# Turning rows by transposing DMAs instead of by TensorE in the Mamba half of a two-part layer

## The chip, the cores and the metric

The kernel runs on one core of a Trainium2 chip. The metric is the device time of one execution in microseconds (us), of which the kernel before has three: median 3758.88, from 3757.54 to 3760.82.

## The reference

An input of 8 sequences of 1024 tokens with 512 features is normalised and goes through two blocks, whose results are added to it. The first is a Mamba-2 block, the second a routed attention that picks 512 queries and 256 keys for each of 4 groups. The change touches only the first:

```python
u = _layernorm(x, ln_w, ln_b)
zxbcdt = u @ in_proj_w.T
...
y = y * jax.nn.silu(z)
y = y * jax.lax.rsqrt(jnp.mean(y * y, -1, keepdims=True) + EPS) * gamma
return x + y @ out_proj_w.T
```

Both matrix products need their left operand with the features on the partitions. The rows, though, are normalised with the tokens on the partitions. So a block of rows is turned (transposed) ahead of each product: `u` ahead of the input projection, and the gated and normalised `y` ahead of the output projection.

## The kernel before

The Mamba half works through 16 blocks of 512 tokens, each of 4 chunks of 128 tokens: 64 chunks in all. Numbers that enter a product in full precision are split into two fp16 tiles, a high and a low part, and the product is the sum of three fp16 products.

For each chunk, `xn` normalises 128 rows, `xh` (ScalarE) and `low` (VectorE) write the two halves of the tile `xh` (128 x 2 x 512, two buffers). `turn` is 8 TensorE transposes of 128 x 128 into a PSUM bank, and `turn_out` a ScalarE copy to `xhT`. When the four chunks of a block are there, `logits`, ten `conv` products (one for each 128 channels, followed by four taps on VectorE) and `z` (two for each chunk) read `xhT`.

The scan itself is done by chunk: `open` turns the convolved channels, `inter` applies the state, `intra` is the product within the chunk, `state` makes the new state. `intra` of chunk ch needs the matrix `de[ch % 2]`, which is a broadcast of the cumulated decays over all partitions, read from DRAM by `bc_in` (1 MB, on the SP queue); `bc_in` of chunk ch waits for `intra` of chunk ch - 2. After `intra` comes a chain over three engines: `y2` and `yz` (VectorE), `square` (ScalarE), `mean` (VectorE), `root` (GpSimd), `y_high` (ScalarE), `y_low` (VectorE). It ends in the tile `yhl` (128 x 2 x 1024 fp16, one buffer). `gate` is 16 TensorE transposes of it into two PSUM banks, `gate_out` a ScalarE copy to `yT` (one buffer), and `proj` the output projection, 24 matrix products that read `yT`.

Every engine works through one fixed list of steps. The list is made before the launch: `make_plan` writes down the order of TensorE steps, and `arrange_steps` gives every step an engine, a duration, the steps that it needs, and an `extra` for what passes until a DMA has landed. `Order.run` then lists the steps of all engines by due time; TensorE may take one of the next four steps (`AHEAD_M`). On the chip nothing is reordered: an engine whose next step lacks its operand waits on a semaphore, and all behind it on that engine waits too. That holds for SP, which only issues DMAs, as well. In the Mamba half its list holds `x_in` (the rows of a block, 1 MB, which waits until `skip_store` of the block before has landed), `skip_store` and `rows_out` (1 MB each, to DRAM), `cum_store` and `bc_in`. Beside it GpSimd issues one accumulating DMA of 256 KB a chunk (`o_add`).

After the Mamba half (to about 1855 us of 3758) come a ranking of tokens and the attention half, in which nothing is changed.

Of the kernel before, what the change touches and what calls it, by code (L numbers as in the profile page):

```python
# [8 lines left out]
F32 = mybir.dt.float32  # L9
# [34 lines left out]
TURNS = CK * 3.45 + 15.23  # L44
CONV_START, CONV_END = -0.05, 1.05
# [318 lines left out]
def chain(*gens):  # L364
# [10 lines left out]
    "turn": [("single", 1, 1.4)],  # L375
# [15 lines left out]
    "turn": [(1.0, "turn_out")],  # L391
# [19 lines left out]
    "turn": lambda i, c: (("low", i, c), 1.5),  # L411
# [39 lines left out]
def arrange_steps(order, line, late):  # L451
# [3 lines left out]
    def last(step):  # L455
        return step if step[1] >= 0 else None
# [8 lines left out]
    for step in line:  # L465
# [3 lines left out]
        elif name == "turn":  # L469
            add("PE", 0.45, step, [("low", a, b)], [("single", [("turn_out", a, b)])])  # L470
        elif name == "logits":
            add("PE", 1.33, step, [("turn_out", a, c) for c in range(CK)] + [("slice_low", 0)], [("single", [("logits_out", a)])])
        elif name == "cum":
            add("PE", 1.9, step, [("dt", a)], [("single", [("cum_copy", a)]), ("single", [("cum_exp", a)])])
        elif name == "conv":
            add("PE", 2.6, step, [("turn_out", a, CK - 1), ("slice_low", PIECE_OF[b])], [("single", [("raw", a, b)])])
# [5 lines left out]
        elif name == "z":  # L482
            add("PE", 3.02, step, [("turn_out", a // CK, CK - 1), ("slice_low", 3 + b), ("bias_get", 3 + b)], [("single", [("z_silu", a, b)])])
        elif name == "gate":
            add("PE", 0.9, step, [("y_low", a)], [("pair", [("gate_out", a)])])
# [4 lines left out]
        elif name == "proj":  # L490
            add("PE", 5.18, step, [("gate_out", a), ("wout_low", KI - 1)], [("single", [("proj_out", a)])])
# [19 lines left out]
    for i in range(NBLK):  # L511
# [8 lines left out]
        for c in range(CK):  # L520
# [8 lines left out]
            add("ACT", 0.58, ("turn_out", i, c), [("turn", i, c)] + [last(("z", CK * (i - 2) + CK - 1, 1))])  # L529
# [18 lines left out]
    for ch in range(NCH):  # L548
# [12 lines left out]
        add("DVE", 1.22, ("dxs", ch), [("open", ch), ("bias_get", len(PIECES) - 1), ("slice_low", len(PIECES) - 1), last(("y2" if opens(ch - 1) else "y_skip", ch - 1))])  # L561
# [22 lines left out]
        add("ACT", 1.0, ("gate_out", ch), [("gate", ch), last(("proj", ch - 1))])  # L584
# [147 lines left out]
def make_plan():  # L732
# [6 lines left out]
    def norms(i):  # L739
        for c in range(CK):  # L740
            yield ("xn", i, c)
            yield Pause(3.0)
            if c:
                yield ("turn", i, c - 1)
                yield 0.6
        yield Pause(2.0)
        yield ("turn", i, CK - 1)
        yield 0.6

    def turns(i):  # L750
        for c in range(CK):
            yield ("turn", i, c)
            yield 0.45
            yield Pause(3.0)
        yield ("logits", i)
        yield 1.33
        yield Pause(12.0)
        yield ("cum", i)
        yield 1.9
# [6 lines left out]
    def back(i):  # L766
        for ch in range(i * CK, (i + 1) * CK):
# [23 lines left out]
            yield ("gate", ch)  # L791
            yield 0.9
# [6 lines left out]
    record.steps += [("slice_bias", 0), ("turn", 0, 0), ("turn", 0, 1), ("turn", 0, 2), ("turn", 0, 3),  # L799
# [100 lines left out]
class Sems:  # L900


    def __init__(self, sem):
        def two(name):
# [12 lines left out]
        self.turned, self.xT, self.skip_out, self.row_out = (sem(s) for s in ("x_turned", "xT", "skip_out", "row_out"))  # L917
# [18 lines left out]
        self.yh, self.yl, self.yt_mm, self.yT, self.o_mm, self.o = (  # L936
            sem(s) for s in ("y_high", "y_low", "y_turned", "yT", "o_mm", "o"))
# [22 lines left out]
def program(nc, x, w_in, ln_w, ln_b, conv_w, conv_b, a_log, d_skip, dt_bias, gamma, w_out,  # L960
            w_route, wq, wkv, wo, null_k, null_v, null_tok, consts, out):
    ctx = ExitStack()
    with ctx:
# [158 lines left out]
        def staged(g, k):  # L1122
# [19 lines left out]
            "turn": lambda i, c: [(S.xT, CK * i + c + 1)],  # L1142
# [6 lines left out]
            "gate": lambda ch: [(S.yT, ch + 1)],  # L1149
# [42 lines left out]
        def tensor_engine():  # L1192
# [25 lines left out]
            def turn(i, c):  # L1218
                q.wait_ge(S.xl, CK * i + c + 1)
                wait_given_back(q, "turn", i, c)  # L1220
                b16 = bank("turn", i, c)[:].bitcast(F16)
                for j in range(2 * KD):
                    ins = pe.transpose(b16[:, j * P:(j + 1) * P], xh[c % 2][:, j // KD, (j % KD) * P:(j % KD + 1) * P], id16[:])
                ins.then_inc(S.turned, 1)
# [1322 lines left out]
```

## Time and profile before

| | before |
|---|---|
| median of three runs | 3758.88 us |
| profiled execution | span 3758.3 us; the page gives no other time for it, and the median of the runs is 0.6 us above |
| Mamba half | 0 to 1855 us, 64 chunks |
| steady period (two blocks, 8 chunks) | 225.4 us |
| TensorE, VectorE, ScalarE busy in that period | 220.05, 198.31, 164.43 us |
| granted TensorE clock in that period | 1.00 of 2.4 GHz |

Busy time is the time in which at least one instruction of the engine was running. In the steady state the picture repeats every two blocks, so that one period of 225.4 us (900.1 to 1125.5 us, chunks 28 to 35) stands for the rest; the half has eight of them, less what differs at its two ends.

### The profile page before, as it was taken

The page shows a single profiled execution, that of the slowest core. Times are in us where ns is not written, and L with a number is a line of the kernel's source. Part 1 is how long each engine was busy: PE and PEld are TensorE (multiplying, and loading weights), DVE is VectorE, ACT ScalarE, POOL GpSimd, SP SyncE. Part 2 cuts the span into 40 slices and gives each one's busy share as a digit, 9 for nine tenths or more (in the row PEclk, how much of TensorE's full clock was granted, in tenths as well). Part 3 has the DMA queues.
Part 4 walks back from the last instruction along what each step waited for, and adds up shares of the span by engine and source line. Part 5 has one row for each costly group of instructions (what it writes and reads, how often), then busy time and mean ns, then how long its engine had stood idle before and what let it go on. Part 6 is the DMA issues. An engine that isn't in the chain of part 4 may idle for free.

```text
span 3758.3 us, 72452 instructions
## 1 busy us (share of the span) xinstructions
PE 3570.5 (95%) x28408; PEld 2173.2 (58%) x28408; DVE 2968.7 (79%) x5336; ACT 2534.8 (67%) x4777; POOL 1858.1 (49%) x1483
## 2 busy tenths in 40 slices
PE   7899999999999999999869999999999999999998
PEld 4555555555555555555435566556666566666665
DVE  6898988988889888988978777786777777677764
ACT  6677676777777767775637666676666766666665
POOL 1332333333333333332337887876665765666565
PEclk9899999999999999999979999999999999999999
DMA  4233322233332332322354343444333533333332
GB/s 144 60 89 79 87 58 74 69 88 79 79 77 65 77 80 77 85 60 55 73 86 119 63 82 69 75 106 86 73 79 69 111 80 76 71 74 78 74 68 38
DMA packets 297669, 294.29 MB, mean 78 GB/s; under 512 B 38663, under 2 KB 222087, under 8 KB 295280
## 3 DMA queue, kind: packets, MB, share of 16 engines
q1 hardware_dynamic: 241008, 186.70, 19.8%
q0 software_dynamic: 56320, 102.94, 15.4%
q8 instruction: 226, 3.70, 0.4%
q14 instruction: 115, 0.94, 0.1%
HBM read 176.19 MB, written 101.71 MB: 74 GB/s over the span
## 4 chain that ended last, share of the span: by engine, by line
PE 64%; DVE 14%; ACT 3%; issue 3%; DMA 2%; POOL 1%; another core or an unknown queue 0%; SPq 0%; ACTq 0%; DVEq 0%
PE pair L1384 8%; PE pair L1499 6%; PE pair L1336 6%; PE pair L1250 5%; PE pair L1298 5%; PE pair L1399 4%; PE pair L1413 4%; PE pair L1346 3%; PE pair L1460 3%; PE pair L1459 3%; PE pair L1429 2%; DVE cv L1649 2%; PE pair L1480 2%; PE pair L1478 2%; PE pair L1488 2%
## 5 line engine op out<-in xcount | busy, mean ns | idle before, releaser
L2345 POOL TENSOR_TENSOR ph<-pf,ph 128x512 f16<-128x512 f32 x256 | 381.7, 1492 | 319.2 <-ACT ph L2208 316.4
L1649 DVE SCALAR_TENSOR_TENSOR cv<-raw,taps,cv 128x512 f32<-128x512 f32 x480 | 417.7, 892 | 19.7 <-ACT cv L2062 18.0
L1903 DVE TENSOR_REDUCE smx<-pair 128x2 f32<-128x514 f32 x512 | 349.9, 685 | 82.1 <-PE pair L1429 79.1
L1250 PE MATMUL pair<-xhT,whi 128*128 128x512 f16 x1280 | 382.0, 380 | 5.8 <-DVE dts L1607 5.7
L1298 PE MATMUL pair<-zhi,xhT 128*128 128x512 f16 x1024 | 331.4, 385 | 13.7 <-DVE yb L1727 10.7
L2202 ACT ACTIVATE pf<-pair 128x1024 f32<-128x1024 f32 x256 | 262.1, 1024 | 96.0 <-PE pair L1460 92.2
L1336 PE MATMUL pair<-ohi,yT 128*128 128x512 f16 x1024 | 320.2, 384 | 3.3 <-ACT yT L2120 3.3
L2092 ACT ACTIVATE de<-de,cum 128x128 f32<-128x128 f32 x1024 | 311.2, 388 | 1.1
L1938 DVE TENSOR_TENSOR ph<-pf,ph 128x512 f16<-128x512 f32 x256 | 232.2, 908 | 99.4 <-ACT ph L2208 98.2
L2208 ACT CAST ph<-pf 128x1024 f16<-128x1024 f32 x256 | 267.9, 1047 | 4.4
L1346 PEld LDWEIGHTS pair<-xdt,de 128*128 128x128 f32 x2048 | 250.7, 201 | 17.8 <-issue 10.6
L1346 PE MATMUL pair<-xdt,de 128*128 128x64 f32 x2048 | 249.6, 283 | 9.3 <-issue 5.6
L2350 POOL TENSOR_TENSOR ohl<-of,ohl 128x256 f16<-128x256 f32 x256 | 200.8, 793 | 86.0 <-ACT ohl L2213 83.9
L1865 DVE SCALAR_TENSOR_TENSOR qa<-pair,qa 64x512 f16<-64x512 f32 x256 | 176.5, 689 | 84.5 <-ACT qa L2173 79.2
L1250 PE MATMUL pair<-xhT,wlo 128*128 128x512 f16 x640 | 243.1, 380 | 0.0
L2339 POOL DMA_INDIRECT y<-res,slot_i x128 | 214.0, 1672 | 51.7 <-ACT res L2227 31.9
L1480 PE MATMUL pair<-vhi,ph 128*128 128x65 f16 x2048 | 238.3, 194 | 0.0
L1478 PE MATMUL pair<-vhi,ph 128*128 128x65 f16 x2048 | 238.3, 194 | 0.0
L1479 PE MATMUL pair<-vlo,ph 128*128 128x64 f16 x2048 | 237.8, 193 | 0.0
L2318 POOL DMA_INDIRECT gat<-rows,slot_i x192 | 193.8, 1009 | 63.1 <-issue 28.7
L2276 POOL TENSOR_TENSOR yb<-yb,dxs 128x1024 f32<-128x1024 f32 x56 | 150.4, 2685 | 141.2 <-DVE yb L1700 139.8
L1476 PE MATMUL pair<-nvb,pnT 96*128 96x65 f16 x1024 | 200.3, 196 | 11.4 <-ACT xq L2165 7.3
(273 smaller groups left out, 10462.2 us busy)
## 6 DMA issues: line engine op xcount, KB each, us to landing
de<-cum SPq DMA_DIRECT2D x64, 1024.0 KB, 9.4
rows<-rowt SPq DMA_DIRECT2D x16, 1040.0 KB, 4.2
xin<-x SPq DMA_DIRECT2D x16, 1024.0 KB, 13.6
y<-xin SPq DMA_DIRECT2D x16, 1024.0 KB, 4.3
y<-ob POOLq DMA_DIRECT2D x64, 256.0 KB, 4.4
qb<-qa SPq DMA_DIRECT2D x32, 512.0 KB
rbc<-rank SPq DMA_DIRECT2D x63, 256.0 KB
wst<-wkv SPq DMA_DIRECT2D x32, 256.0 KB
```

The source lines that it names most:

```text
L1250: ins = pe.matmul(bk[:], w[:, k, ws], xt[:, ha, k, :], start=n == 0, stop=n == 3 * KD - 1)
L1298: pe.matmul(pz[:], xt[:, ha, k, cs], w[:, k, j * 512:(j + 1) * 512], start=n == 0, stop=False)
L1336: ins = pe.matmul(bk[:], yT[:, ha * KI + k, :], w[:, k, :], start=k == 0 and n == 0, stop=k == KI - 1 and n == 2)
L1346: ins = pe.matmul(pw[:, h * HD:(h + 1) * HD], de[ch % 2][:, h, :], xdt[:, h, :], start=True, stop=True)
L1384: ins = pe.matmul(bk[:], w[:, k, ws], xq[:, ha * KD + k, :], start=n_ == 0, stop=n_ == 3 * KD - 1)
L1478: pe.matmul(o, p_[:, 0, j, qs_], vhi[u][:, j, h, :], start=False, stop=False, skip_group_check=True)
L1480: ins = pe.matmul(o, p_[:, 1, j, qs_], vhi[u][:, j, h, :], start=False, stop=j == KT - 1, skip_group_check=True)
L1649: ve.scalar_tensor_tensor(c_[:], r_[:, t:t + BLK], taps[:, ct, t:t + 1], c_[:], ALU.mult, ALU.add).then_inc(done, 1)
L1903: ve.tensor_reduce(smx[:, qt, 2 * h2:2 * h2 + 2], sc[:, :, 0:NK + 1], AX.X, ALU.max)
L2092: ins = ac.activation(d_[:, h, :], d_[:, h, :], ACT.Relu, bias=cum_t[i % 2][:, c, h:h + 1], scale=-1.0)
L2208: ac.copy(p_[:, 0], f[:]).then_inc(S.ph, 1)
L2345: po.tensor_tensor(p_[:, 1, 1], f[:, 1], p_[:, 0, 1], ALU.subtract).then_inc(S.plp, 1)
```

## The change

The steps `turn` and `gate` move from TensorE to SP. Each is now one transposing DMA from SBUF to SBUF: of `xh`, 128 x 1024 fp16 (256 KB), to `xhT`; and of `yhl`, 128 x 2048 fp16 (512 KB), to `yT`. The 64 x 8 and 64 x 16 TensorE transposes, the PSUM banks that they used, and the ScalarE copies `turn_out` and `gate_out` are gone. Who waited for a transpose or a copy now waits for the landing of the DMA: `xh` for the transposing DMA of two chunks before, `square` for that of the chunk before, `logits`, `conv` and `proj` for their operands. Two waits that the old steps implied are written out (`xdt` for `xw`, `gram_out` for `mask`). The planner is told that issuing takes 0.6 us, and landing a further 4.0 and 5.0 us; the lists of all engines are made anew from that.

```diff
+TURN_ISSUE, TURN_LANDS, GATE_LANDS = 0.6, 4.0, 5.0
...
-        elif name == "turn":
-            add("PE", 0.45, step, [("low", a, b)], [("single", [("turn_out", a, b)])])
...
-        elif name == "gate":
-            add("PE", 0.9, step, [("y_low", a)], [("pair", [("gate_out", a)])])
...
-            add("PE", 5.18, step, [("gate_out", a), ("wout_low", KI - 1)], [("single", [("proj_out", a)])])
+            add("PE", 5.18, step, [("gate", a), ("wout_low", KI - 1)], [("single", [("proj_out", a)])])
...
-            add("ACT", 0.58, ("turn_out", i, c), [("turn", i, c)] + [last(("z", CK * (i - 2) + CK - 1, 1))])
+            add("SP", TURN_ISSUE, ("turn", i, c), [("low", i, c), last(("z", CK * (i - 2) + CK - 1, 1))], extra=TURN_LANDS)
...
-        add("ACT", 1.0, ("gate_out", ch), [("gate", ch), last(("proj", ch - 1))])
+        add("SP", TURN_ISSUE, ("gate", ch), [("y_low", ch), last(("proj", ch - 1))], extra=GATE_LANDS)
...
             def conv(i, ct):
-                q.wait_ge(S.xT, CK * (i + 1))
+                for j in range(2):
+                    q.wait_ge(S.xT[j], 16 * CK // 2 * (i + 1))
...
             def proj(ch):
-                q.wait_ge(S.yT, ch + 1)
+                q.wait_ge(S.yT, 16 * (ch + 1))
...
+                q.wait_ge(S.xw, kept(ch))
...
             def gram_out(ch):
                 q.wait_ge(S.g, ch + 1)
+                q.wait_ge(S.m, ch)
...
             def xh_(i, c):
                 ch = CK * i + c
                 q.wait_ge(S.xn, ch + 1)
-                q.wait_ge(S.turned, ch - 1)
+                q.wait_ge(S.xT[c % 2], 16 * (ch // 2))
...
             def square(ch):
                 q.wait_ge(S.yz, ch + 1)
-                q.wait_ge(S.yt_mm, ch)
+                q.wait_ge(S.yT, 16 * ch)
...
-            def gate_out(ch):
-                q.wait_ge(S.yt_mm, ch + 1)
-                q.wait_ge(S.o_mm, ch)
-                ac.copy(yT[:].bitcast(F32).rearrange("p j t -> p (j t)"), bank("gate", ch)[:]).then_inc(S.yT, 1)
...
+            def turn(i, c):
+                q.wait_ge(S.xl, CK * i + c + 1)
+                q.wait_ge(S.z_mm, 2 * CK * (i - 1))
+                sp.dma_start_transpose(xhT[i % 2][:].rearrange("p h k t -> p (h k) t")[:, :, c * P:(c + 1) * P],
+                                       xh[c % 2][:].rearrange("p h d -> p (h d)")).then_inc(S.xT[c % 2], 16)
+
+            def gate(ch):
+                q.wait_ge(S.yl, ch + 1)
+                q.wait_ge(S.o_mm, ch)
+                sp.dma_start_transpose(yT[:], yhl[:].rearrange("p h d -> p (h d)")).then_inc(S.yT, 16)
```

How the lists of steps change shows at two places. The first is the SP list about chunks 29 to 33. `de<-cum` is `bc_in`, `rows<-rowt` is `rows_out`, `cum<-cumT` is `cum_store`, `xhT<-xh` is `turn` and `yT<-yhl` is `gate`. Of the kernel before (`bc_in` of chunks 29 to 33):

```order
L2408 DMA de<-cum 128x16x128
L2389 DMA xin<-x 128x4x512
L2398 DMA rows<-rowt 128x4x520
L2408 DMA de<-cum 128x16x128
L2402 DMA cum<-cumT 16x512
L2408 DMA de<-cum 128x16x128 x2
L2393 DMA y<-xin 128x4x512
L2408 DMA de<-cum 128x16x128
```

Of the changed kernel (`bc_in` of chunks 30 to 33, `gate` of chunks 28 to 31, the four `turn` of block 9):

```order
128 L2371 DMA de<-cum 128x16x128
129 L2361 DMA rows<-rowt 128x4x520
130 L2352 DMA_TRANSPOSE yT<-yhl 128x16x128
131 L2365 DMA cum<-cumT 16x512
132 L2371 DMA de<-cum 128x16x128
133 L2352 DMA_TRANSPOSE yT<-yhl 128x16x128
134 L2371 DMA de<-cum 128x16x128
135 L2346 DMA_TRANSPOSE xhT<-xh 128x8x128 x2
136 L2352 DMA_TRANSPOSE yT<-yhl 128x16x128
137 L2346 DMA_TRANSPOSE xhT<-xh 128x8x128 x2
138 L2371 DMA de<-cum 128x16x128
```

Between two `bc_in` there now stand one `gate` and, in one gap of each block, up to four `turn` as well. In six of the blocks `x_in` (`xin<-x`) comes right behind a `bc_in`, with the next `gate` behind both; this is the place at `bc_in` of chunks 17 and 18, with `gate` of chunk 15:

```order
80 L2346 DMA_TRANSPOSE xhT<-xh 128x8x128 x2
81 L2356 DMA y<-xin 128x4x512
82 L2371 DMA de<-cum 128x16x128
83 L2341 DMA xin<-x 128x4x512
84 L2352 DMA_TRANSPOSE yT<-yhl 128x16x128
85 L2361 DMA rows<-rowt 128x4x520
86 L2371 DMA de<-cum 128x16x128
```

The second place is ScalarE, in the changed kernel, from `square` of chunk 30 (row 929) to the last two `xh` of block 9 (rows 944 and 947), which wait for the first two `turn` of SP row 135:

```order
936 L2071 ACTIVATE yhl<-yb,yn 128x1024
937 L2018 ACTIVATE cv<-raw,conv_bias,taps 128x512
938 L2060 ACTIVATE zs<-pair 128x512
939 L1971 CAST rowt<-xn 128x512
940 L1996 ACTIVATE xsT<-cv 128x512
941 L1981 ACTIVATE xin<-xin,nrm 128x512
942 L2076 ACTIVATE ob<-pair 128x512
943 L2038 COPY btok<-pair 128x128
944 L1977 ACTIVATE xh<-xn,nrm 128x512
945 L1966 ACTIVATE xn<-xin,nrm 128x512
946 L1996 ACTIVATE xsT<-cv 128x512
947 L1977 ACTIVATE xh<-xn,nrm 128x512
```

In the kernel before, the third `xh` of that block waited for TensorE alone; now it stands some ten instructions behind `y_high` of chunk 30 (row 936) and waits for a DMA.

## Rows read from the trace of the kernel before

**Rows 1.** The page: busy time and share by engine; granted clock in slices.

```profile
PE 3570.5 (95%) x28408; PEld 2173.2 (58%) x28408; DVE 2968.7 (79%) x5336; ACT 2534.8 (67%) x4777; POOL 1858.1 (49%) x1483
...
PEclk9899999999999999999979999999999999999999
```

**Rows 2.** Busy time by stretch: Mamba half, one steady period, the ranking behind.

```profile
0.00:1855.00 1855.00, 1770.38 (x10763) 1043.77 (x10764) 1599.06 (x2248) 1318.54 (x2933) 598.71 (x393) 0.98 0.32 78
900.10:1125.50 225.40, 220.05 (x1365) 128.62 (x1363) 198.31 (x268) 164.43 (x366) 76.02 (x49) 1.00 0.32 76
1855.00:2020.00 165.00, 121.15 (x802) 72.20 (x801) 131.19 (x257) 77.79 (x131) 77.33 (x68) 0.80 0.49 93
```

**Rows 3.** Waits of TensorE, 200 to 1800 us: first and last of eleven.

```profile
PE pair L1298 <- DVE yb L1727: 10.7, 5, 2.1
...
PE pair L1307 <- DVE dxs L1684: 0.2, 1, 0.2
```

**Rows 4.** Timeline about one `gate` (L1307) and one `turn` (L1223).

```profile
930.37 1.06 PE L1307 MATMUL pair<-id,yhl 128*128 128x128 f16 x16
931.26 0.59 PE L1250 MATMUL pair<-xhT,whi 128*128 128x512 f16 x2
931.46 1.01 ACT L2120 COPY yT<-pair 128x1024 f32<-128x1024 f32 x1 [3.60 <-PE pair L1307]
...
985.53 0.61 PE L1223 MATMUL pair<-id,xh 128*128 128x128 f16 x8
985.97 0.71 PE L1275 MATMUL pair<-cst,xsT 128*128 128x128 f32 x5
```

**Rows 5.** Groups of ScalarE in the Mamba half: the two copies.

```profile
L2120 ACT COPY yT<-pair 128x1024 f32<-128x1024 f32 x61 | 61.5, 1008 | 64.0 <-PE pair L1307 63.7
L2025 ACT COPY xhT<-pair 128x512 f32<-128x512 f32 x64 | 36.6, 573 | 7.3 <-PE pair L1223 7.3
```

**Rows 6.** Timeline: `intra` (L1346) of chunk 28, three `y_low` (L1741), their `proj` (L1336).

```profile
914.49 3.68 PE L1346 MATMUL pair<-xdt,de 128*128 128x64 f32 x32
927.58 1.28 DVE L1741 SCALAR_TENSOR_TENSOR yhl<-yb,yn,yhl 128x1024 f16<-128x1024 f32 x1
934.84 0.38 PE L1336 MATMUL pair<-ohi,yT 128*128 128x512 f16 x1
...
1013.49 1.28 DVE L1741 SCALAR_TENSOR_TENSOR yhl<-yb,yn,yhl 128x1024 f16<-128x1024 f32 x1
1021.96 0.38 PE L1336 MATMUL pair<-ohi,yT 128*128 128x512 f16 x1
...
1120.43 1.28 DVE L1741 SCALAR_TENSOR_TENSOR yhl<-yb,yn,yhl 128x1024 f16<-128x1024 f32 x1
1130.56 0.39 PE L1336 MATMUL pair<-ohi,yT 128*128 128x512 f16 x1
```

**Rows 7.** DMA, 200 to 1800 us: SP's queue; issues with KB, us to landing.

```profile
q1 hardware_dynamic: 140800, 103.98, 24.1%
...
de<-cum SPq DMA_DIRECT2D x57, 1024.0 KB, 9.4
...
rows<-rowt SPq DMA_DIRECT2D x14, 1040.0 KB, 4.2
...
xin<-x SPq DMA_DIRECT2D x13, 1024.0 KB, 13.6
...
cum<-cumT SPq DMA_DIRECT2D x14, 32.0 KB, 1.6
```

**Rows 8.** Timeline of SP: a `bc_in`, an `x_in`; landing of all `x_in`.

```profile
886.95 0.36 SPq L2408 DMA_DIRECT2D de<-cum  x1
887.35 1.92 SPq L2389 DMA_DIRECT2D xin<-x  x1
...
DMA to landing us min/median/max: 5.1/13.6/15.1
```

**Rows 9.** Waits in the first 150 us: TensorE for `low` of block 0.

```profile
PE pair L1223 <- DVE xh L1596: 18.5, 5, 5.0
```

More of the change, by code:

```diff
@@ L468, in arrange_steps @@
             add("PE", 4.9 if a > 2 else 3.5, step, [("slice_in", a)], [("single", [("bias_get", a)])])
-        elif name == "turn":
-            add("PE", 0.45, step, [("low", a, b)], [("single", [("turn_out", a, b)])])
         elif name == "logits":
-            add("PE", 1.33, step, [("turn_out", a, c) for c in range(CK)] + [("slice_low", 0)], [("single", [("logits_out", a)])])
+            add("PE", 1.33, step, [("turn", a, c) for c in range(CK)] + [("slice_low", 0)], [("single", [("logits_out", a)])])
         elif name == "cum":
@@ L475, in arrange_steps @@
         elif name == "conv":
-            add("PE", 2.6, step, [("turn_out", a, CK - 1), ("slice_low", PIECE_OF[b])], [("single", [("raw", a, b)])])
+            add("PE", 2.6, step, [("turn", a, CK - 1), ("slice_low", PIECE_OF[b])], [("single", [("raw", a, b)])])
         elif name == "gram":
@@ L737, in feed @@
         return Feed(gen, total, plan, alone)
[L739 to L748, printed above, removed]
     def turns(i):
[L751 to L754, printed above, removed]
+        yield Pause(CK * 3.45)
         yield ("logits", i)
@@ L1241, in conv @@
             def conv(i, ct):
[L1242 removed]
+                for j in range(2):
+                    q.wait_ge(S.xT[j], 16 * CK // 2 * (i + 1))
                 q.wait_ge(S.wlo_m, PIECE_OF[ct] + 1)
@@ L1300, in z @@
                 pe.matmul(pz[:], ones[:], z_bias[:, j * 512:(j + 1) * 512], start=False, stop=True).then_inc(S.z_mm, 1)
-            def gate(ch):
-                q.wait_ge(S.yl, ch + 1)
-                wait_given_back(q, "gate", ch)
-                pt16 = bank("gate", ch)[:].bitcast(F16)
-                for j in range(2 * KI):
-                    ins = pe.transpose(pt16[:, j * P:(j + 1) * P], yhl[:, j // KI, (j % KI) * P:(j % KI + 1) * P], id16[:])
-                ins.then_inc(S.yt_mm, 1)
             def inter(ch):
@@ L2478, in stored @@
                     q.wait_ge(S.res_out[j], 16 * ITEMS * QT // 2)
-            does = {"prep": prep, "slice_in": slice_in, "wout_in": wout_in, "x_in": x_in,
+            does = {"prep": prep, "slice_in": slice_in, "wout_in": wout_in, "x_in": x_in, "turn": turn, "gate": gate,
                     "skip_store": skip_store, "rows_out": rows_out, "cum_store": cum_store, "bc_in": bc_in,
```

43 lines of the change are left out of this document (11 added, 32 removed).

## The prediction

> **What bounds the kernel now.** I read the page first: TensorE is busy for 95% of the span, VectorE for 79%, ScalarE for 67%, and nearly every slice has the full clock [rows 1]. Then busy time by stretch, since the change touches only the Mamba half: there TensorE is busy 1770 of 1855 us. In one steady period it is 220.05 of 225.4 us, VectorE 198.31 (88%) and ScalarE 164.43 (73%), at a granted clock of 1.00 [rows 2]. Third, who TensorE waits for: the longest of eleven releasers costs 10.7 us in 1600, the shortest 0.2, and all eleven together 35 us [rows 3]. So TensorE is the bound, and what is taken from it is gained, as long as the thing that takes its place is not late; VectorE is the next bound, 27 us of idle time per period behind.
>
> **What is removed.** The end of a busy time is modelled, so I price a step by the distance from its start to the start of the next TensorE step. A `gate` starts at 930.37 and its follower at 931.26: 0.89 us. A `turn` starts at 985.53, its follower at 985.97: 0.44 us [rows 4]. There are 64 of each: 64 x (0.89 + 0.44) = 85 us. ScalarE loses 64 copies of 1.008 us and 64 of 0.573 us [rows 5], 101 us; it waits a lot already, and this makes room and does not count by itself.
>
> **What it costs VectorE.** Its work stays 198.3 us, while the period would fall by 8 x 1.33 = 10.6 us to 214.8: its idle time falls from 27.1 to 16.5 us [rows 2]. TensorE's own idle time is 5.35 us per period now. If that grows as VectorE's idle time shrinks, it becomes 5.35 x 27.1 / 16.5 = 8.8 us, 3.4 more. The freed banks and ScalarE's room work against that, so I take half: 1.7 x 8 periods = +14 us (ends: 0 and +28).
>
> **How long the transposing DMAs take.** No row shows one. Below: the smallest DMA of SP, 32 KB, lands in 1.6 us, and 1040 KB go out in 4.2 us, so 1008 KB cost 2.6 us; by bytes `gate` (512 KB) is 1.6 + 1.3 = 2.9 us, and `turn` (256 KB) 2.3. Above, as an estimate: `bc_in` writes 128 x 16 = 2048 runs of 512 B, and `gate` has 2048 runs of 256 B if it is cut into runs of 128 elements. SP's queue took 24.1% of 16 engines in 1600 us for 140800 packets, 43.8 ns each, so 2048 of them are 5.6 us on 16 engines, and the other 3.8 of the 9.4 us are the fixed part. By runs `gate` takes 9.4 us, and `turn` with half as many 6.6 [rows 7]. A transpose has to write narrow pieces, so it is nearer to `bc_in`: I take 7.0 and 5.0 us, plus 0.36 us to issue (as `bc_in`, rows 8).
>
> The pages pull both ways. The Trainium skill ("Advanced Engine Details and Errata", X-Bar Transpose) has transposing DMAs as fast as plain ones, 350 to 400 GB/s; by it `gate` would be at my lower end. The Trainium skill ("VectorE: DVE Perf Modes", the three transpose paths) has 1309 ns for 128 x 128 by DMA against 390 by TensorE, and advises TensorE where PSUM will do; 16 such tiles in a row would be 20.9 us, and the sum below would end near 4500 us. No row here decides between them.
>
> **What hides it.** What matters is how long after the end of `y_low` its `proj` starts. In the period of [rows 6] the eight distances are 5.98, 6.86, 9.39, 7.19, 6.44, 9.37, 14.55 and 8.85 us (first, fourth and last stand there: 927.58 + 1.28 = 928.86 to 934.84, and so on). TensorE works on other steps meanwhile, so these are slack. A landing after 7.4 us is late by 1.42, 0.54, 0.21 and 0.96 us in four of eight: 3.1 us per period, 25 us in all. At 9.8 us seven are late by 14.5 us in sum: 116 us in all. At 3.3 us none is. The new list helps a little: the TensorE steps between `intra` and `proj` of a chunk, 16.4 us or more in the old list, are 17.7 or more in the new one (estimates, with step durations of this trace). I take +15 of the 25.
>
> **What stands in SP's queue.** SP's DMAs go out one behind another: the `x_in` issued 0.4 us behind a `bc_in` is one of thirteen whose median landing is 13.6 us, while the quickest took 5.1 [rows 8]; 13.6 is about 9.4 + 4.2. `bc_in` is issued when `intra` ends, at 918.2 in [rows 6]; `y_low` ends 10.7 us later, just behind its landing. So a lone `gate` meets an empty queue, and that cover is thin. (a) In six blocks `x_in` stands between the two: it lands 14.0 us after `bc_in` was issued, `gate` is 3.3 us later. Less the slack of some: +10 us. (b) In most blocks two `turn` go out right behind a `bc_in` with a `gate` behind them (SP rows 134 to 136 in the change). Two transfers of 1.6 us (half of 7.0 less the fixed 3.8) end 12.6 us after the issue, so `gate` is 1.9 us later in some 14 blocks, of which slack hides half: +12 us. (c) Behind these `turn` wait the third and fourth `xh` on ScalarE: row 944 is reached some 13 us after `intra`, the first `turn` lands at about the same time. If it is later, `raw`, `decs` and `de` behind it on ScalarE are late, and with them `mask` and the next `intra`. At 5.0 us I take nothing. (d) SP now waits for `y_low` ahead of the next `bc_in`; that one is needed a chunk later (28 us), and costs nothing. (e) `square` waits for the `gate` before, 24 us earlier: nothing. (f) The written-out waits of `xdt` and `gram_out` are for steps long done: nothing.
>
> **The start.** TensorE waits 18.5 us for `low` in block 0 [rows 9]; now a landing follows each, the last uncovered: +5 us.
>
> **Sum.** -85 + 14 + 15 + 10 + 12 + 5 = -29 us, from the profiled 3758.3 (0.6 below the median of the runs): about 3730 us, 0.8% faster. The likeliest case alone: 3690 to 3755.
>
> **Rivals.**
> 1. *The landing is short* (3 to 4 us): no distance is missed, the queue terms vanish. -85 + 14 + 5 and some 6 of queueing = -60: 3699 us. For it: bytes by [rows 7]. Chance 0.15.
> 2. *The transposes run by runs like `bc_in`, or a little worse.* 116 less 20 for the new order, queue terms doubled to 45: -85 + 14 + 96 + 45 + 5 = +75: about 3833 us, with 3750 to 3890 around it. It decides from a landing of about 8.5 us on. For it: the run count; against: half the bytes. Chance 0.21.
> 3. *The transposes go tile after tile instead of 16 at a time.* Sixteen tiles at 1.6 us, what the smallest DMA takes [rows 7], are 25.6 us. Every `proj` waits: 139 us per period by the eight distances, 1114 us in all, about 4800 us; half as long a landing (13.2 us) still adds some 300, about 4000 us. Past 24 us `square` waits too, as `yhl` has one buffer. The clock may add to it: behind the Mamba half, where TensorE is busy for 121 of 165 us, the granted clock is 0.80 [rows 2]. By the second of the two pages this is the case to expect. Chance 0.18.
> 4. *VectorE is already the bound.* If its 27 us of idle time per period can't shrink, the period stays 225 us and only waits move: 3759 us. Against it: TensorE's waits are 35 us in 1600 [rows 3]. Chance 0.08.
>
> My forecast keeps 0.38. A change of less than 0.2% (7.5 us) can't be told from none here. Faster: 0.35 of the forecast, 0.15 of rival 1 and 0.01 of rival 2: 0.51. Within 0.2%: 0.02, rival 4 and 0.02 of rival 2: 0.12. Slower: 0.01, 0.18 and 0.18: 0.37. The range of 3680 to 3890 takes in rival 2 and leaves 0.18 above it and 0.02 below.
>
> **What will show it.** The issue table gives `gate` and `turn` with us to landing: 7.0 and 5.0, or not; this alone decides most. TensorE's waits should name the DMA `yT` as what `proj` waits for, 20 to 60 us in sum, and the DMA `xhT` with next to nothing. The steady period should be near 222 us (225.4 less 29 / 8), TensorE busy 209.5 of it, VectorE 198. ScalarE's wait for the `turn` DMA ahead of `xh` should be small. A clock below 1.00 in the steady state, or an SP issue of some us for each transpose, would break the sum: SP would then be late with `bc_in` as well.

## The result, and the profile after

The changed kernel takes 3690.69 us (median of four runs, 3684.36 to 3697.4) beside 3759.85 us of the kernel before (four runs, 3757.54 to 3766.13). The ratio is 0.9816, with a 95% interval of 0.9801 to 0.9831: 1.8% faster, some 69 us. The forecast was 3730 us: the direction was right, and the gain is 2.4 times the 29 us that it had. One of four executions of a kernel below (`gate` alone) took 7336.86 us, twice the others, and is left out of its median and ratio.

The page of the changed kernel: span; busy time, share and instructions by engine; granted clock in slices.

```profile
span 3690.6 us, 69594 instructions
...
PE 3470.4 (94%) x26872; PEld 2075.7 (56%) x26872; DVE 2934.9 (80%) x5336; ACT 2445.5 (66%) x4649; POOL 1871.1 (51%) x1483
...
PEclk9899999999999999999879999999999999999999
```

Against [rows 1] TensorE has lost 100 us and 1536 matmuls (64 x 24), ScalarE 89 us. VectorE has lost 34 us with the same number of instructions. Two of its groups in the Mamba half became shorter, by 29 us each: `low`, and the product that ends the SiLU behind the convolution (`xsT`). Their medians are as before (0.75 and 0.68 us); there are fewer long cases (of up to 2.9 us). Why, no run here shows. The first line of each pair is the kernel before:

```profile
L1596 DVE SCALAR_TENSOR_TENSOR xh<-xn,nrm,xh 128x512 f16<-128x512 f32 x64 | 90.4, 1413 | 30.0 <-ACT xh L2014 30.0
L1557 DVE SCALAR_TENSOR_TENSOR xh<-xn,nrm,xh 128x512 f16<-128x512 f32 x64 | 61.7, 965 | 6.7 <-ACT xh L1977 6.4
...
L1655 DVE SCALAR_TENSOR_TENSOR xsT<-xsT,cv 128x512 f32<-128x512 f32 x160 | 157.2, 987 | 32.8 <-ACT xsT L2040 32.5
L1616 DVE SCALAR_TENSOR_TENSOR xsT<-xsT,cv 128x512 f32<-128x512 f32 x160 | 128.2, 813 | 9.4 <-ACT xsT L1996 8.0
```

Busy time by stretch (columns as in [rows 2]): the Mamba half, 220 us of the steady state, and the ranking behind.

```profile
0.00:1820.00 1820.00, 1708.40 (x9400) 968.28 (x9401) 1600.70 (x2303) 1247.76 (x2842) 626.60 (x402) 0.98 0.49 108
900.00:1120.00 220.00, 217.45 (x1213) 122.56 (x1212) 199.22 (x281) 153.13 (x352) 88.94 (x53) 1.00 0.48 106
1820.00:1990.00 170.00, 116.07 (x907) 69.35 (x906) 129.00 (x265) 85.16 (x136) 90.53 (x82) 0.84 0.58 111
```

The DMA share has gone from 0.32 to 0.49. To place the gain I take the stretch from the start of the first `intra` to the start of the last (63 chunks on), before and after:

```profile
111.60:1899.30 1787.70, 1722.91 (x10512) 1011.47 (x10512) 1566.61 (x2165) 1260.26 (x2816) 599.39 (x388) 0.98 0.31 75
111.70:1820.10 1708.40, 1636.72 (x9039) 922.30 (x9040) 1525.05 (x2146) 1174.80 (x2688) 609.85 (x387) 0.98 0.48 106
```

TensorE was busy for 1722.9 us and idle for 64.8; now it is busy for 1636.7 and idle for 71.7. So its busy time fell by 86 us, its idle time grew by 7, and the stretch is 79 us shorter. From the last `intra` to the end it is the other way round: 1859.1 us before, 1870.5 after, so that some 12 us are given back there in this profile. In the profile of the same kernel once more (below) it is 1863.7, so only part of the 12 us is sure.

The clock did change. It has two levels, 1.00 (2.4 GHz) and 0.50 (1.2 GHz), and this is 200 to 1700 us in the profiles before, after, and with `gate` alone:

```profile
200.00:1700.00 1500.00, 1467.13 (x9122) 1.00 0.31 76
200.00:1700.00 1500.00, 1457.60 (x8141) 0.99 0.49 108
200.00:1700.00 1500.00, 1476.06 (x8564) 1.00 0.43 98
```

The clock records behind these means show it finer: the lower level was granted for 14 us in all before, for 37 us after (again 37 in the repeated run), and for 10 us with `gate` alone (14 in its repeated run). Each of the seven falls of the changed kernel comes during a wait of TensorE of 2 to 6 us or within 1.3 us of its end.

DMA between 200 and 1750 us: SP's queue, and issues with KB and median us to landing.

```profile
q1 hardware_dynamic: 319625, 149.62, 41.4%
...
de<-cum SPq DMA_DIRECT2D x58, 1024.0 KB, 9.5
...
xin<-x SPq DMA_DIRECT2D x13, 1024.0 KB, 9.2
...
yT<-yhl SPq DMA_TRANSPOSE x57, 4.3
xhT<-xh SPq DMA_TRANSPOSE x54, 3.8
```

Here is the row that the forecast said would decide most: `gate` lands in 4.3 us where 7.0 was taken, and `turn` in 3.8 where 5.0 was. `bc_in` still takes 9.5, and `x_in` has gone from 13.6 [rows 7] to 9.2, as it is issued 4.8 us or more behind a `bc_in` in 12 of 13 cases, where it was 0.4 us behind in 11 of 13. The same two steps by line, with the time that an issue keeps SP (min/median/max in ns), who waited for them, and the spread of the landings:

```profile
L2352 SPq DMA_TRANSPOSE yT<-yhl x57: 1322/1894/3949, 218.3 to 1723.2; - x57
...
  PE pair L1297: 12.3, 3
...
DMA to landing us min/median/max: 4.2/4.3/10.4
```
```profile
L2346 SPq DMA_TRANSPOSE xhT<-xh x54: 1232/1296/6160, 204.4 to 1610.4; - x54
...
  ACT xh L1977: 1.9, 1
...
DMA to landing us min/median/max: 2.7/3.8/10.0
```

The landing counts from the start of the issue, so the 1.9 us of issuing are within the 4.3. One `gate` in the timeline, from the end of `y_low` (1807.46 + 1.27) to the first matmul of `proj`, shows that: issued at 1808.76, read at 1813.07, 4.31 us later.

```profile
1807.46 1.27 DVE L1704 SCALAR_TENSOR_TENSOR yhl<-yb,yn,yhl 128x1024 f16<-128x1024 f32 x1
...
1808.76 1.79 SPq L2352 DMA_TRANSPOSE yT<-yhl  x1
...
1813.07 0.61 PE L1297 MATMUL pair<-ohi,yT 128*128 128x512 f16 x1 [11.44 <-DMA yT<-yhl]
...
1838.37 0.61 PE L1297 MATMUL pair<-ohi,yT 128*128 128x512 f16 x1 [14.61 <-DMA yT<-yhl]
...
1869.36 2.81 PE L1332 MATMUL pair<-id,gat 128*128 128x128 f16 x24 [22.19 <-DMA gat<-rows,slot_i]
```

The two `proj` here are the last of the half. TensorE has little else to do and waits 11.4 and 14.6 us. The landing is 4.3 us of each wait; the rest is the chain from `intra` to `y_low`, with no other work beside it. Then TensorE runs at 0.61 us a matmul where [rows 6] has 0.38: the granted clock was 0.50 from 1806.5 to 1816.7 and from 1827 to 1844 us. Only the second wait lies behind the last `intra` (1820.1), where the 12 us are. There the last landing (4.3 us) and the slow `proj` (8.2 us where 5.2 is usual) stand on the chain of work that ended last. Who TensorE waits for over the whole half (us in total, times, longest):

```profile
PE pair L1297 <- DMA yT<-yhl: 38.3, 5, 14.6
PE pair L1204 <- issue: 23.9, 6, 11.8
```

Of the 38.3 us for `yT`, 26.0 are those two chunks; the other 62 chunks cost 12.3 us, of which 11.9 are two waits. In both of these, SP had issued `bc_in`, `x_in` and then `gate`, and the `gate` landed only after 10.4 and 9.9 us:

```profile
536.62 0.51 SPq L2371 DMA_DIRECT2D de<-cum  x1
541.82 1.23 SPq L2341 DMA_DIRECT2D xin<-x  x1
548.46 3.95 SPq L2352 DMA_TRANSPOSE yT<-yhl  x1
...
558.87 0.61 PE L1297 MATMUL pair<-ohi,yT 128*128 128x512 f16 x1 [6.14 <-DMA yT<-yhl]
```

The second row is `logits` (L1204), which can start only when all four `turn` of a block have landed. Behind block 0 it waits for another 12.1 us in all, 9.1 of them at two places where the last `turn` of a block was issued some 2 us behind a `bc_in` and landed after 8.4 and 8.3 us:

```profile
315.45 0.37 SPq L2371 DMA_DIRECT2D de<-cum  x1
317.36 4.32 SPq L2346 DMA_TRANSPOSE xhT<-xh  x1
...
325.81 0.18 PE L1204 MATMUL pair<-shi,xhT 128*128 128x24 f16 x1 [4.56 <-issue]
```

The longest wait for `logits`, 11.8 us, is that of block 0 and stands where the 18.5 us of [rows 9] stood; the first `intra` starts at 111.7 us, as it did before (111.6).

### The profile page after: what moved, and what is told of

Its sections match the earlier page's. It is cut to its first block, busy times and chain, and to the rows that moved or that the text cites. A ratio compares the mean times of both kernels' runs of the same rounds, so it can differ in the third digit from the quotient of the medians.

```text
span 3690.6 us, 69594 instructions
## 1 busy us (share of the span) xinstructions
PE 3470.4 (94%) x26872; PEld 2075.7 (56%) x26872; DVE 2934.9 (80%) x5336; ACT 2445.5 (66%) x4649; POOL 1871.1 (51%) x1483
## 4 chain that ended last, share of the span: by engine, by line
PE 69%; DVE 14%; DMA 4%; issue 4%; ACT 3%; POOL 1%; another core or an unknown queue 0%; DVEq 0%; ACTq 0%
PE pair L1345 8%; PE pair L1297 7%; PE pair L1219 7%; PE pair L1460 6%; PE pair L1267 6%; PE pair L1360 4%; PE pair L1307 4%; PE pair L1374 4%; PE pair L1421 3%; PE pair L1420 3%; PE pair L1390 2%; PE pair L1278 2%; PE pair L1287 2%; PE pair L1441 2%; PE pair L1332 2%
## 5 line engine op out<-in xcount | busy, mean ns | idle before, releaser
L1610 DVE SCALAR_TENSOR_TENSOR cv<-raw,taps,cv 128x512 f32<-128x512 f32 x480 | 429.0, 921 | 27.8 <-ACT cv L2018 26.5
L1297 PE MATMUL pair<-ohi,yT 128*128 128x512 f16 x1024 | 322.5, 387 | 39.1 <-DMA yT<-yhl 38.3
L2153 ACT ACTIVATE pf<-pair 128x1024 f32<-128x1024 f32 x256 | 262.1, 1024 | 92.3 <-PE pair L1421 88.3
L1307 PEld LDWEIGHTS pair<-xdt,de 128*128 128x128 f32 x2048 | 239.7, 193 | 16.7 <-issue 8.7
L1307 PE MATMUL pair<-xdt,de 128*128 128x64 f32 x2048 | 237.7, 275 | 3.8 <-DVE dxs L1646 3.8
L2231 POOL TENSOR_TENSOR yn<-yn,neghalf 128x1 f32<-128x1 f32 x64 | 48.7, 760 | 350.3 <-DVE yn L1700 350.1
L1219 PEld LDWEIGHTS pair<-xhT,whi 128*128 128x128 f16 x1280 | 123.8, 99 | 168.9 <-issue 35.2
```

What stands on the lines that cost most here:

```text
L1219: ins = pe.matmul(bk[:], w[:, k, ws], xt[:, ha, k, :], start=n == 0, stop=n == 3 * KD - 1)
L1297: ins = pe.matmul(bk[:], yT[:, ha * KI + k, :], w[:, k, :], start=k == 0 and n == 0, stop=k == KI - 1 and n == 2)
L1307: ins = pe.matmul(pw[:, h * HD:(h + 1) * HD], de[ch % 2][:, h, :], xdt[:, h, :], start=True, stop=True)
L1610: ve.scalar_tensor_tensor(c_[:], r_[:, t:t + BLK], taps[:, ct, t:t + 1], c_[:], ALU.mult, ALU.add).then_inc(done, 1)
L2153: ac.activation(f[:].rearrange("p k q -> p (k q)"), bank("score", n, h)[:], ACT.Exp, scale=SCALE).then_inc(S.pf, 1)
```

## The experiments

Each ratio is against the kernel before on the same chip, with its 95% interval. Where two kernels are compared I take the difference of their ratios times 3760 us; an interval is some 6 us to either side, so a difference under about 8 us is not settled (12 where `gate` lands later with the lists not told of it: there the interval is 9 to 10 us to either side).

### One step alone

The first kernel keeps `gate` as a DMA and has `turn` and `turn_out` of the kernel before; the second is the reverse. The lists are made anew for each.

```diff
-                sp.dma_start_transpose(xhT[i % 2][:].rearrange("p h k t -> p (h k) t")[:, :, c * P:(c + 1) * P],
-                                       xh[c % 2][:].rearrange("p h d -> p (h d)")).then_inc(S.xT[c % 2], 16)
+                for j in range(2 * KD):
+                    ins = pe.transpose(b16[:, j * P:(j + 1) * P], xh[c % 2][:, j // KD, (j % KD) * P:(j % KD + 1) * P], id16[:])
```

> Only `gate` is a DMA, `turn` is back on TensorE and ScalarE. If the gain is the TensorE time removed (0.89 us for each of 64 gates, 57 us), less a few us of waits: 3705 to 3718. If the gain came from the emptier lists of ScalarE or from freed banks, no fixed share is expected; ScalarE loses 65 of the 101 us here, which would give about 3715 as well, so that this run alone does not tell the two apart.

> Only `turn` is a DMA. TensorE time removed: 64 x 0.44 = 28 us; with the landings of `turn` hidden: 3732 to 3742. If the `turn` landings hold up ScalarE at `xh`, as the forecast feared, or SP is late with `bc_in`: 3760 or more.

Measured: `gate` alone 3680.36 us (median of three), 0.9813 (0.9793 to 0.9833); `turn` alone 3713.84 us, 0.9893 (0.9876 to 0.9909). So `gate` alone gives 70 us and `turn` alone 40, and both together 69. Each alone gives more than I expected, and more than the TensorE time that it removes (57 and 28 us). They do not add up: on top of `gate`, moving `turn` gives nothing. The same kernel once more, beside the unaltered changed kernel on one chip:

> The kernel with only `gate` by DMA once more: 3685. If `turn` by DMA adds nothing on top of `gate` by DMA, it is within 0.3% of the changed kernel beside it; if engine time freed always counts (28 us of TensorE, 37 of ScalarE, at their prices some 20 us), it should be slower by 20 us.

> The changed kernel once more, unaltered, on the same chip as the two beside it: 3690, within 0.2%. It shows how far a repetition alone moves.

3686.36 us, 0.9806 (0.9792 to 0.9819), and 3689.96 us, 0.9817 (0.9804 to 0.9831): the same again. The stretch from first to last `intra` shows how it comes about. With `gate` alone it is this:

```profile
115.90:1816.30 1700.40, 1648.32 (x9447) 942.44 (x9443) 1551.41 (x2149) 1198.40 (x2746) 609.62 (x387) 0.99 0.43 97
```

TensorE is busy for 1648.3 us and idle for 52.1; with both it is busy for 1636.7 and idle for 71.7. Moving `turn` takes only 12 us off TensorE's busy time, and 20 us of idle time come back. In the half with `gate` alone, the wait for block 0 and that for `yT` look like this:

```profile
PE pair L1207 <- DVE xh L1572: 21.3, 5, 7.2
PE pair L1312 <- DMA yT<-yhl: 14.8, 5, 10.7
```

14.8 us for `yT` against 38.3. Between 200 and 1700 us it is 2.6 against 12.3, and `logits` waits for 0.3 us, against 12.1: these are the waits behind `bc_in` and `x_in` shown above. With them go 37 us at the lower clock against 10. TensorE does its work at half pace there, so that, as an estimate, up to (37 - 10) / 2 = some 13 us more of its busy time are the same work done slower. Together this is about what `turn` was worth. It was not tested by a run that changes only the order on SP at these places; the lists of the two kernels differ everywhere.

### The engines' work put back

In the changed kernel, with its lists and its DMAs, I put back the TensorE work alone: 24 transposes of 128 x 128 a chunk, into the bank of `z` ahead of its products, where nothing reads them.

```diff
             def z(ch, j):
...
+                pz16 = pz[:].bitcast(F16)
+                for m in range(12):
+                    pe.transpose(pz16[:, m % 8 * P:(m % 8 + 1) * P], id16[:], id16[:])
```

> The changed kernel with 12 spare TensorE transposes of the identity ahead of each `z` product, 24 a chunk, which nobody reads: TensorE's time is given back, ScalarE's is not. Theory that TensorE's time is the gain: back to 3755 to 3785 (3691 + 64 x 24 x 0.0555 = 85 us). Rival that ScalarE's room and the freed banks made it: stays under 3715.

Then ScalarE's alone: three copies of 128 x 512 a chunk.

```diff
             def z_tanh(ch, j):
...
+                for _ in range(2 - j):
+                    ac.copy(zs[:, j * 512:(j + 1) * 512], bank("z", ch, j)[:]).then_inc(*own.up())
+                    q.wait_ge(*own.now())
```

> The changed kernel with three spare ScalarE copies a chunk of a `z` bank (0.58 us each, 111 us in all; 101 were removed), each waited for by ScalarE itself. Theory that TensorE's time is the gain: 3691 to 3710. Rival that ScalarE's room made it: 3730 to 3760.

And both together:

> The changed kernel with both the spare TensorE transposes and the spare ScalarE copies. Alone they cost 46 and 27 us (ratios 0.9939 and 0.9887 against 0.9816). If the two are all there is in the gain and add up: 3755 to 3775. If the freed PSUM banks, the new lists or the absent wait of TensorE for ScalarE's copy are worth something by themselves: 3725 to 3745. If they cross: under 3735.

The groups show that the work is there (TensorE between 200 and 1700 us; ScalarE in the whole run):

```profile
L1267 PE MATMUL pair<-id 128*128 128x128 f16 x1308 | 90.8, 219 | 0.3 <-DVE zs L1659 0.3
```
```profile
L2061 ACT COPY zs<-pair 128x512 f32<-128x512 f32 x192 | 110.9, 578 | 11.0 <-PE pair L1269 8.9
```

Measured: TensorE's work back 3730.13 us, 0.9939 (0.9923 to 0.9956), 46 us above the changed kernel; ScalarE's back 3716.43 us, 0.9887 (0.9868 to 0.9907), 27 us above; both back 3762.58 us, 0.9997 (0.9986 to 1.0009), 68 us above, which is the size of the whole gain. 46 + 27 = 73 agrees with 68 within the intervals. I had expected the first to return all of it (3755 to 3785), and the second little or nothing (3691 to 3710): both were wrong. The transposing DMAs run in all three kernels, and the lists are those of the changed kernel. So at fixed lists the time of the two engines is worth about 0.54 us for each of TensorE's 85, and 0.24 for each of ScalarE's 111.

That this is the whole gain is not shown. The lists were not told of the spare work, and the order of the lists alone is worth some 20 us (below). VectorE's work did not come back: it is busy for 192.7 us in eight chunks with both works put back, where it was 197.2 before and is 191.7 in the changed kernel. The lower clock did go: 7 us between 200 and 1700 us with both put back and 10 with TensorE's work alone, against 37, which makes the spare work look cheaper than it is. And the two prices do not give the kernels with one step moved: by them `gate` would be worth 0.54 x 57 + 0.24 x 65 = 46 us and `turn` 0.54 x 28 + 0.24 x 37 = 24, where 70 and 40 were measured.

### VectorE, which the change leaves alone

`xdt` (1.22 us on VectorE) is computed twice in each chunk, in the changed kernel and in the kernel before.

```diff
+                ve.tensor_tensor(xdt[:], p3, dt_t[i % 2][:, c, :].unsqueeze(2).to_broadcast([P, NH, HD]), ALU.mult).then_inc(*own.up())
+                q.wait_ge(*own.now())
```

> The changed kernel with `xdt` computed twice on VectorE (1.22 us a chunk, 78 us in all). Theory that after the change VectorE is a bound beside TensorE (TensorE's time given back cost only half, so TensorE alone is not it): +35 to +70 us, 3725 to 3760. Theory that TensorE alone bounds: under +15, 3705.

> The same spare work in the kernel before. If TensorE was the bound there and VectorE had 27 us of idle time per period, as the forecast read it: +0 to +20 us, 3760 to 3780. If VectorE's wait chain counted there already: +35 to +70.

The doubled instruction in the kernel before:

```profile
L1677 DVE TENSOR_TENSOR xdt<-pair,dt 128x1024 f32<-128x1024 f32 x63 | 77.1, 1224 | 2.2
```

In the changed kernel it costs 48 us (3739.12 us, 0.9944, 0.9928 to 0.996), in the kernel before 41 (3801.76 us, 1.0108, 1.0091 to 1.0125), for 78 us put in: 0.62 and 0.53 a us. The two can't be told apart. So VectorE's 27 us of idle time in a period of 225 took up only about half of the work put in, in either kernel. The price is that of work at this place, ahead of `intra`, with lists that are not told of it.

### A later landing

A first transposing DMA, whose landing SP awaits, is put ahead of `gate`: of one 128 x 128 tile, then of all 16.

```diff
+                sp.dma_start_transpose(yT[:, 0:1, :], yhl[:].rearrange("p h d -> p (h d)")[:, 0:1 * P]).then_inc(S.yT0, 16)
+                q.wait_ge(S.yT0, 16 * (ch + 1))
                 sp.dma_start_transpose(yT[:], yhl[:].rearrange("p h d -> p (h d)")).then_inc(S.yT, 16)
```

> Each `gate` is issued only when a first transposing DMA, of one 128 x 128 tile of the same rows, has landed; so `yT` is there some 7 us after `y_low` and not 4.3. This is the landing that the forecast took. Slack read from the changed kernel's own trace (64 distances from `y_low` to `proj`, 4.34 to 11.5 us) is missed by 26 us in sum at 7.2 us: 3710 to 3725. The forecast's own sum for this landing was 3730. If the landing is not what set the time (rival: the forecast's terms for VectorE and for SP's queue were too high, and the landing mattered little): under 3700.

> The same with a first DMA of all 16 tiles, so that `yT` lands twice as late, at 8.7 us or so. By the distances, missed by 78 us in sum: 3755 to 3785. Rival that the landing mattered little: under 3720. Rival 2 of the forecast had 3833 for 9.8 us.

SP in the first of them, one `gate`; then TensorE's wait for `yT` in the half, in the first and in the second:

```profile
1027.24 1.13 SPq L2352 DMA_TRANSPOSE yT<-yhl  x1
1029.58 1.33 SPq L2354 DMA_TRANSPOSE yT<-yhl  x1
```
```profile
PE pair L1297 <- DMA yT<-yhl: 65.6, 20, 17.0
```
```profile
PE pair L1297 <- DMA yT<-yhl: 132.7, 52, 15.7
```

From `y_low` to `yT` it is now some 6.7 us with one tile (3724.57 us, 0.9902, 0.9874 to 0.9929: 32 us slower than the changed kernel), and some 8.9 with sixteen (median; 8.6 at least; 3845.82 us, 1.0218, 1.0193 to 1.0243: 151 us slower, and slower than the kernel before). The first comes close to the landing that the forecast assumed for `gate` (7.0 + 0.36 us; `turn` stays short), and 3724.57 us is near its 3730. The second is well above what I expected (3755 to 3785). The distances from `y_low` to `proj` in the changed kernel's timeline, 64 of them, are missed by 17 us in sum at 6.7 us and by 78 at 8.7. The runs gave about twice that. Only 27 and 94 us of it are in the wait for `yT`. The stretch from first to last `intra` shows more. The changed kernel stands above (1708.40 us, TensorE busy for 1636.72); here are the one with one tile and the one with sixteen:

```profile
111.80:1853.10 1741.30, 1645.66 (x9039) 925.07 (x9040) 1525.23 (x2150) 1175.76 (x2688) 611.21 (x387) 0.97 0.48 105
111.90:1962.90 1851.00, 1674.79 (x9038) 930.18 (x9039) 1521.80 (x2153) 1177.88 (x2688) 609.82 (x387) 0.96 0.54 116
```

TensorE's idle time grows by 24 and 104 us. Its busy time grows as well, by 9 and 38 us, with the same matmuls: the lower clock was granted for 48 and 102 us between 200 and 1700 us, where it was 37. So a quarter of what the late landing costs in this stretch is TensorE at the lower clock. Of the idle time, the part that is not in the wait for `yT` was not taken apart; SP is held for the first landing too, and so everything behind it in its list is later.

Then the same first DMA, with lists that are told of it (`GATE_LANDS` 6.7 instead of 5.0):

> The late `gate` (7 us, through a first DMA of one tile) with lists that are told of it (0.6 + 6.7 in place of 0.6 + 5.0). If a landing of 7 us can be hidden by another order: 3690 to 3705, in place of 3725. If the chain from `intra` to `proj` is simply too long for the work that is there: 3715 to 3730.

3693.2 us, 0.982 (0.9807 to 0.9834). TensorE's wait for `yT`:

```profile
PE pair L1297 <- DMA yT<-yhl: 26.7, 7, 12.7
```

The same later landing costs 32 us if the lists are not told. If they are, the kernel is as fast as the changed kernel; against the kernel with the same lists and the short landing (0.9795, the last one below) it is 0.0025 or 9 us slower, at the edge of what can be told.

### The lists alone

`GATE_LANDS`, `TURN_LANDS` and the time of issuing only decide in which order the engines' fixed lists are written. First the measured values (issue 1.8 and landing 2.5 for `gate`, 1.25 and 2.5 for `turn`, block 0 left as it was), with both steps as DMAs and with `gate` alone; then wide ones (1.8 and 5.5, 1.25 and 5.0); then 0.6 and 6.0 with `gate` alone; last 0.6 and 6.7 for `gate` in the changed kernel.

```diff
-TURN_ISSUE, TURN_LANDS, GATE_LANDS = 0.6, 4.0, 5.0
+TURN_ISSUE, TURN_LANDS, GATE_ISSUE, GATE_LANDS = 0.6, 4.0, 0.6, 6.7
...
-        add("SP", TURN_ISSUE, ("gate", ch), [("y_low", ch), last(("proj", ch - 1))], extra=GATE_LANDS)
+        add("SP", GATE_ISSUE, ("gate", ch), [("y_low", ch), last(("proj", ch - 1))], extra=GATE_LANDS)
```

> The changed kernel with lists made from the measured DMA times (`turn` 1.25 us to issue and 2.5 more to land, `gate` 1.8 and 2.5, from block 1 on) in place of 0.6 + 4.0 and 0.6 + 5.0. The work is the same. Theory that `turn` by DMA costs some 8 us of waits on top of `gate` by DMA only because the lists leave SP and the landing out of step: 3670 to 3685, faster than the only-gate kernel. Rival that the two together are at a floor set by VectorE: 3685 to 3700, no change.

> Only `gate` by DMA, lists made from its measured times. If lists matter little: 3675 to 3695, the same as the only-gate kernel (3685). If they are a lottery of their own: anything 15 us off.

> Both by DMA, lists made as if they landed late (`turn` 1.25 + 5.0, `gate` 1.8 + 5.5). Work and landings are the same. It measures how far the lists alone move the time: 3680 to 3700 if little. If TensorE's waits for `xhT` ahead of `logits` (12 us in the steady state) were the price of `turn` by DMA, they vanish and it gains about as much: 3675 to 3685.

> Only `gate` by DMA, with lists made as if it landed after 0.6 + 6.0 us; it lands after 4.3 in all. If a margin in the lists is what pays (the late landing told to the lists lost nothing, the lists with the tight measured times lost 29 us): 3670 to 3690. If the lists are only a lottery: anywhere from 3680 to 3715.

> The changed kernel, with lists made as if `gate` landed after 0.6 + 6.7 us: the lists of the late gate that was told, without its first DMA. If a margin ahead of `proj` is worth more than tightness: 3675 to 3690 (faster than the changed kernel beside it). If the time hangs on the lists only by chance and the landing is hidden either way: within 10 us of the late gate's 3693.

| lists | us | ratio (95%) |
|---|---|---|
| both steps, as measured | 3697.57 | 0.9842 (0.9829 to 0.9856) |
| `gate` alone, as measured | 3713.57 | 0.9875 (0.986 to 0.989) |
| both steps, wide | 3698.74 | 0.984 (0.9826 to 0.9853) |
| `gate` alone, 0.6 + 6.0 | 3701.2 | 0.984 (0.9823 to 0.9858) |
| both steps, `gate` 0.6 + 6.7 | 3682.02 | 0.9795 (0.9778 to 0.9812) |

With the same steps on every engine the ratio goes from 0.9795 to 0.9842 with both steps (18 us), and from 0.9806 and 0.9813 to 0.9875 with `gate` alone (23 to 26 us). The true durations give worse lists than the wrong ones, by 10 and 23 to 26 us, and the wider margins except the last are slower by 9 to 13 us as well. The last is the fastest kernel of all here, 2.05% below the kernel before; beside the changed kernel on the same chip it is 0.2% faster, with intervals that overlap.

## Why the prediction came out as it did

**The step that failed: how long the transposing DMAs take.** The forecast took 7.0 and 5.0 us, between an end by bytes (2.9 and 2.3) and an end by runs (9.4 and 6.6), "nearer to `bc_in`". They took 4.3 and 3.8. The landings count the issue. The number of runs was right: between 200 and 1700 us the queue carried 177,568 packets more than before, of which 6,144 belong to three more `bc_in`, and 55 `gate` of 2048 and 54 `turn` of 1024 make 167,936.

Two prices were wrong. The first is that of a run: the queue's share rose from 24.3% to 41.4% of 16 engines in those 1500 us, 4104 us for 177,568 packets, or 23 ns each. The forecast had 43.8, but that is the mean over all packets of the queue. In the trace the 512 B packets of `bc_in` took 36.3 ns before and 34.4 after, and the 256 B packets of the transposes 23.5 (21.3 where a `gate` ran alone). The second, and for the total as large, is the fixed part of 3.8 us, which was `bc_in`'s landing less its runs. A `gate` that runs alone has its first packet 1.2 us after the start of the issue, its packets take 2.6 us, and it has landed 0.5 us later: 1.7 us beside the runs. With 3.8 it would have been 6.4 us, still near the forecast. The packets of a `bc_in`, for their part, take 3.5 to 4.9 us of 16 engines and are mostly spread over about 8, so that its landing is not engine time plus a fixed part. The issue was put at 0.36 us and takes 1.9 and 1.3; it is within the landing.

The two pages fare as follows. By the Trainium skill ("Advanced Engine Details and Errata", X-Bar Transpose) a transposing DMA is as fast as a plain one. The trace does not agree for the rate: the packets of a `gate` alone move 512 KB in 2.6 us, some 200 GB/s, and those of a `rows_out` alone 1040 KB in 2.9 us, some 370. By the Trainium skill ("VectorE: DVE Perf Modes", the three transpose paths) 128 x 128 takes 1309 ns by DMA; the trace does not agree for 16 tiles in one DMA, 0.27 us each, nor for one tile by itself, which was there after 2.3 us (the run with one tile ahead of `gate`).

**What hangs on it.** With the short landing the term +15 (missed slack) has next to nothing left to price: apart from two waits behind `x_in`, TensorE waits for `yT` for 0.4 us in all between 200 and 1700 us. The two queue terms did not vanish. `x_in` ahead of `gate` (+10) cost 11.9 us of waits in two blocks. `turn` ahead of `gate` (+12) cost `proj` nothing, but `turn` behind `bc_in` kept `logits` waiting for 9.1 us, a place where the forecast saw no cost. The run with nearly the landing that the forecast assumed gave 3725 us, 32 above the changed kernel, where the three terms are 31 above the 6 of rival 1. The size is right, but only the landing of `gate` was moved there, and the two queue terms are for other places than those where the trace shows waits, so part of the agreement is luck. Rival 1's case, -85 + 14 + 5 + 6 = -60 and 3699 us, is 8 above what was measured. Rival 2's case was reached by the run with sixteen tiles ahead of `gate`: with 8.9 us behind `y_low` the kernel is 82 us slower than before, where the forecast had it break even at 8.5 and 75 us slower at 9.8. Between the points at 6.7 and 8.9 it would break even at some 7.4 us (an estimate, on a straight line), so the forecast held a late landing too cheap; the lower clock, a quarter of the cost above, was in no term of its rival 2. The later landing costs less once the lists are told of it, which the forecast did not count: it took the slack of the old lists as given, when the planner makes it.

**TensorE's work, -85 us.** As busy time it was right: 86 us are gone. As a price it was too high, and ScalarE's 101 us at nothing were too low: 46 and 27 us by the runs with the work put back at fixed lists. The two errors nearly cancel, so that -85 is near the 69 us for a wrong reason. The second step that failed is this one: ScalarE's time "does not count by itself". Rival 4 (VectorE is already the bound) was wrong as the case in which nothing is gained, and right in that VectorE's time counts: over half a us for each us, before the change too. So "TensorE is the bound, VectorE the next" was the wrong reading of [rows 2, 3]: work on each of three engines costs time.

**VectorE's idle time, +14 us.** TensorE's idle time in the half grew by 7 us for all causes together, and from 5.2 to 5.8 us in eight chunks (chunks 8 to 56). That VectorE's work stays the same did not hold: it fell from 197.2 to 191.7 us in eight chunks, by the shorter groups above. At the measured 0.5 to 0.6 this would be worth some 20 us of the gain (an estimate), which no term had.

**The start, +5 us.** The first `intra` starts when it did before: nothing. The longer tail at the other end, 12 us and 5 in the two profiles, was in no term; an uncovered landing and a `proj` at the lower clock are in it.

**The signs.** The table of issues decided, as foretold. TensorE's wait for `yT` is 38.3 us in sum (20 to 60 foretold), but 26.0 of it in the last two chunks. ScalarE waits 1.9 us for `xhT`, but TensorE 12.1 us at `logits` behind block 0. The clock was not 1.00 throughout, as shown above. Eight chunks take 215.5 us on average between chunks 8 and 56, where 225.2 stood before and the forecast had 222; TensorE is busy for 209.7 of them, and 209.5 was foretold. An issue of some us was named as something that would break the sum: it is 1.9 and 1.3 us, and up to 6.2 behind a `bc_in`. SP mostly waits all the same, and what it cost beyond the waits above is not shown. SP's longest waits, 200 to 1750 us:

```profile
SPq L2352 <- DVE yhl L1704: 379.0, 52, 13.8
SPq L2371 <- PE pair L1307: 365.6, 47, 17.4
```

**Left open.** How the 69 us divide. Why `turn`, worth 40 us alone, adds nothing on top of `gate` is known in part: with both, TensorE waits some 20 us more for the two landings, and has the lower clock for 27 us more. Whether another order on SP would give that back was not tested. The lists alone move either kernel by 18 to 26 us, which is as much as is missing, so it may be no more than less lucky lists; a run that keeps the order of all other steps while `turn` moves was not made.

## What to carry to other kernels

Where engines follow fixed lists and three of them are busy for 70 to 95% of the time, it need not be that a single one is the bound: here each us of spare work cost a fraction (0.54 on TensorE, 0.5 to 0.6 on VectorE, 0.24 on ScalarE). Spare work put into each engine in turn shows what idle times do not, but its prices hold for that place and those lists, and did not give the worth of one step moved. Beside the landing of a transfer by itself, look at what stands ahead of it in its queue: here two transfers behind a `bc_in` and an `x_in` made up nearly all of the waits for `yT` before the last chunks. The same lateness that costs 32 us untold costs 9 at most if the lists are made with it. And when an engine waits more, its clock can fall too: read the granted clock over the whole stretch, not over one period. Lists made anew from other numbers move such a kernel by 0.5 to 0.7% with no change in its work, so a difference of that size between two versions is not yet an effect of the edit.

## What the runs showed of the hardware

- A transposing DMA of 512 KB from SBUF to SBUF lands in 4.3 us (median; 4.2 at best), one of 256 KB in 3.8 (2.7 at best). One 128 x 128 tile was there 2.3 us after its issue began, so most of a small one is a fixed part. Alone, one of 512 KB has its first packet after 1.2 us, packets for 2.6, and has landed 0.5 us later.
- Issuing one keeps SP for 1.9 us (`gate`) and 1.3 us (`turn`), against 0.36 us for a plain DMA of 1 MB [rows 8]. The longest took 3.9 and 6.2 us.
- A packet of 256 B took 23.5 ns of a DMA engine's time, one of 512 B of `bc_in` 34.4 in the same stretch (200 to 1700 us).
- Behind a `bc_in`, or a `bc_in` and an `x_in`, the landing went up to 10.4 us (`gate`) and 10.6 (`turn`).
- At a granted clock of 0.50 matmuls of `proj` took 0.61 us instead of 0.38. The clock fell to that level during or just behind waits of TensorE: of 2 to 6 us in the steady state of the changed kernel, of 11 and 15 at its end. It was granted for 37 us of 1500 there, for 102 with the latest landing, and for 14 before.
